# A fused Mamba, expert and attention kernel: closing norm and router gate moved to PSUM banks, and transposed sums taken first

## The chip, the cores and the metric

The kernel runs on one core of a Trainium2 chip. The metric is the device time of one execution in microseconds (us). PE is TensorE (matmuls), DVE is VectorE, ACT is ScalarE, POOL is GpSimd, and SP is SyncE, whose queue issues the DMAs.

## What is computed

The input is 8 sequences of 1024 tokens with 256 features. Four layers follow one another, each on a layer norm of its input and added to it: a Mamba block, a mixture of 16 experts, a linear attention, and the same mixture of experts again.

```python
def selective_scan(x_conv, delta, A, Bm, Cm, D_param):
    def step(h, inp):
        dA = jnp.exp(jnp.clip(dt[..., None] * A, -10.0, 0.0))
        h = dA * h + dt[..., None] * bt[:, None, :] * xt[..., None]
        hn = jnp.clip(jnp.linalg.norm(h, axis=-1, keepdims=True), 1e-06, None)
        scale = jnp.where(hn > 10.0, 10.0 / hn, jnp.ones_like(hn))
        h = jnp.where(t % 16 == 15, h * scale, h)      # the bound
        y = jnp.einsum('bn,ben->be', ct, h) + D_param * xt
...
out = (selective_scan(...) * _silu(z)) @ out_proj_w.T + out_proj_b
return layernorm(residual + out, norm_alpha, norm_bias)  # the closing norm

# mixture of experts
probs = jax.nn.softmax(logits, axis=-1)
top_p, top_i = jax.lax.top_k(probs, TOP_K)             # 6 of 16
gate = gate.at[...].add(top_p / (sum(top_p) + EPS))
for e in range(16):
    out = out + x @ expert_w[e] * gate[:, e:e + 1]
```

Of the state, 512 channels with 16 values each are carried from token to token, so the 1024 tokens of a sequence are scanned in order.

## The kernel before

The 8192 tokens are 64 tiles of 128. A first stage takes the tiles through Mamba and the first mixture; a second (`merged`) does attention and both mixtures' remaining work, 64 tiles more. The first is a software pipeline: `step(i, k, stages)` works on tile i's scan, tile i+3's input norm, projections and convolution (stage F), tile i-1's output projection and closing norm (B), tile i-2's router (X_) and tile i-3's experts (Y). Every engine runs its own `step` in the order in which the code is written, and semaphores (`M[...]` for Mamba, `R[...]` for router and experts) hold the engines together. The middle tiles run in a hardware loop.

A step has NC = 8 chunks of 16 tokens. In chunk c, DVE scans (L998, `hb<-ps_dA,hb`); ACT squares the last states (L438), and starts the decays exp(dA) of the next chunk (L432); DVE sums the squares (L1006); ACT makes the factors of the bound (L444, L447); DVE applies them (L1015, L1017, semaphore `hs`). POOL then multiplies the chunk's states with C (L362, `product`, into `prod`) and makes the inputs of the chunk after next (L370, `inputs`, into `hb`), which the scan of that chunk waits for. There are two state buffers `hb`, used in turn. PE turns the products back and adds them up (L706, `sum_states`, into bank G1 as `YT`); ACT copies the sums (L453, `copy_sums`), and PE turns them again into the bank `YP` (L714, `sums_back`), on top of D times x (L751, `skip`).

Around this skeleton each chunk carries other work: in every chunk DVE adds two experts' products to `macc` (L1083) and PE makes the next two (L740, one bank); POOL has a product of 512 columns more in chunks 1, 3 and 5 (L379, L383, L386) and the residual in 7 (L390); ACT makes the decays' arguments (L423), 5 to 11 per chunk.

What the change touches is this. **The closing norm** of tile i-1: in chunk 2 DVE adds the scaled residual to `YP` and writes the SBUF tile `oo` (L1172, `o2`), takes its statistics (L1174, L1177, L1179); in chunk 3 ACT makes the deviation by Ln and Exp (L531, L533, `sd3`), and DVE, behind most of its work of the chunk, adds epsilon, takes the reciprocal and subtracts the mean and multiplies with alpha (L1190, L1197, L1199, `o3`); in chunk 4 it multiplies and adds the bias (L1207, `o4`). **The router** of tile i-2, steps in chunks 4 to 7: the largest eight of `ex` (L1044), their match taken out of `ex` into `rest` (L1053), sums and reciprocals (L1056 to L1065), the difference `selp = ex - rest` (L1070, chunk 6), and `gate` (L1075, chunk 7). **Turning back** of tile i-1's last sums: on PE in chunk 0 behind the transposes of the input norm (L783), on ACT at the end of chunk 0, and on PE in chunk 1 behind the input projection (L794) and the router's transposes (L722).

The chunks' other small items keep their places. PE's `skip` of tile i (L751, chunk 3) writes into `YP` and waits for `o2`, since the closing norm reads that bank.

Of the kernel before, what the change touches and what calls it, by code (L numbers as in the profile page):

```python
# [22 lines left out]
ROUTER = 11  # L23
# [7 lines left out]
def build(nc, dram, out):  # L31
# [3 lines left out]
    with ctx:  # L35
# [118 lines left out]
        nf = trio[:, ST * SL + 16:ST * SL + 16 + EB]  # L154
        G = (G0, G1)
# [252 lines left out]
        def _(a):  # L408
# [65 lines left out]
            def route_init(n, k, x, stored):  # L474

                a.wait_ge(R["router"], AHEAD + n * ROUTER + 9)
# [36 lines left out]
            def step(i, k, stages):  # L513
# [4 lines left out]
                for c in range(NC):  # L518
# [75 lines left out]
                    if c == 0 and B:  # L594
                        copy_sums(i - 1, 1)
# [99 lines left out]
        def _(pe):  # L695
# [66 lines left out]
            def step(i, k, stages):  # L762
# [10 lines left out]
                for c in range(NC):  # L773
                    if early_tile(i, c, 1) is not None:
                        if early_tile(i, c, 1) == 0:
                            pe.wait_ge(M["dtb"], AHEAD + NTILES)
                            pe.wait_ge(M["o2"], AHEAD + NTILES)
                        transposes(early_tile(i, c, 1))
                    if c == 0 and F:
                        pe.wait_ge(M["xn"], AHEAD + i + 3)  # L780
                        pe.wait_ge(M["dtb"], AHEAD + i + 2)
                        for j in range(KD):
                            last = nc.tensor.transpose(F0[:, j * P:(j + 1) * P], xn[:, j * P:(j + 1) * P], ident[:])  # L783
                        last.then_inc(M["xnT"], 1)
                    if c == 0 and B:
                        sum_states(i - 1, 3)
                    if c == 1:
                        if isinstance(i, int) and i == -2:
# [11 lines left out]
                        if B:  # L800
                            sums_back(i - 1, 1)
# [166 lines left out]
        def _(v):  # L968
# [69 lines left out]

            def route_step(n, step):
# [10 lines left out]
                elif step == 3:  # L1050
                    v.wait_ge(R["router"], AHEAD + n * ROUTER + 3)
                    settle()
                    V.match_replace(rest[:], t8[:], ex[:], 0.0).then_inc(R["router"], 1)  # L1053
                elif step == 4:
# [417 lines left out]
```

## Time and profile before

| | before |
|---|---|
| median of 3 runs | 4467.03 us (4465.48 to 4468.92) |
| profiled execution, its own time | 4467.15 us |
| span of its trace | 4465.1 us |
| busy in the span: PE, DVE, ACT, POOL | 88%, 82%, 69%, 58% |
| first and last scan (512 in all) | start at 69.8 and 2968.9 us |

The first stage therefore fills two thirds of the span: 512 scans from 69.8 to 2968.9 us are 5.67 us per chunk and 45.4 us per tile. In it DVE, ACT, POOL and PE are all busy between 86 and 95 parts in a hundred of a typical stretch; an "idle before" in a row names what ended it. In the second stage PE alone is full and POOL does nothing.

### The profile page before, as it was taken

Reading aid. Unit: us, or ns where it says so; the run is one execution under the profiler, and the core shown is the slowest. Engines: PE = TensorE matmul, PEld = TensorE weight load, DVE = VectorE, ACT = ScalarE, POOL = GpSimd, SP = SyncE. Lnnn points to the kernel's source line nnn. Section 1 sums busy time; section 2 is a strip of 40 time slices with the busy share of each in tenths; the row PEclk is TensorE's granted clock in tenths of the full one; section 3 lists DMA queues with packets and bytes.
Section 4 is the critical chain, followed back from the end, with each engine's and each line's share of the span. In section 5 each row is a group of like instructions: output and inputs, shape, how many; then the busy total and the mean of one; then the engine's idle time right before and its main releaser. Section 6 shows DMA issues by size and latency. Waiting matters only on the chain.

```text
span 4465.1 us, 71554 instructions
## 1 busy us (share of the span) xinstructions
PE 3949.8 (88%) x19008; PEld 2583.5 (58%) x19008; DVE 3659.5 (82%) x8418; ACT 3088.2 (69%) x9040; POOL 2599.0 (58%) x1284
## 2 busy tenths in 40 slices
PE   5788888888888888888888888868999999999999
PEld 5666666666666666666666666634454454454454
DVE  4899999999999999999999999974557666666676
ACT  6988888888889888889889898843333333333321
POOL 4988888888889888889888888850000000000000
PEclk8899999999999999999999999999999999999999
DMA  2111111111111111111111111110000000000000
GB/s 108 57 55 56 50 58 54 58 54 58 52 51 59 50 58 54 58 54 58 54 51 56 50 60 53 57 46 15 12 16 8 16 16 6 16 16 7 6 8 10
DMA packets 91266, 187.59 MB, mean 42 GB/s; under 512 B 15873, under 2 KB 57601, under 8 KB 90625
## 3 DMA queue, kind: packets, MB, share of 16 engines
q1 hardware_dynamic: 91136, 186.11, 12.6%
q8 instruction: 52, 0.85, 0.1%
q14 instruction: 78, 0.63, 0.0%
HBM read 168.24 MB, written 17.83 MB: 42 GB/s over the span
## 4 chain that ended last, share of the span: by engine, by line
PE 44%; issue 23%; DVE 16%; POOL 13%; ACT 2%; DVEq 1%; POOLq 0%; ACTq 0%
PE ps L740 24%; POOL prod L362 7%; DVE macc L1083 6%; PE ps L853 5%; POOL hb L370 3%; PE ps L888 3%; PE ps L870 2%; POOL xcv L386 2%; PE ps L706 2%; PE ps L846 1%; POOL u L379 1%; ACT zr L423 1%; PE ps L794 1%; PE ps_dA L888 1%; DVE xin L1194 1%
## 5 line engine op out<-in xcount | busy, mean ns | idle before, releaser
L740 PE MATMUL ps<-w_x,mxT 128*128 128x512 f32 x4096 | 1968.7, 609 | 213.2 <-DVE macc L1083 213.2
L1083 DVE SCALAR_TENSOR_TENSOR macc<-ps,gate,macc 128x256 f32<-128x256 f32 x2048 | 977.9, 478 | 509.7 <-PE ps L740 417.5
L740 PEld LDWEIGHTS ps<-w_x,mxT 128*128 128x128 f32 x4096 | 732.9, 193 | 944.1 <-issue 600.6
L998 DVE TENSOR_TENSOR_SCAN hb<-ps_dA,hb 128x1088 f32<-128x1088 f32 x512 | 1240.1, 2422 | 36.3 <-POOL hb L370 30.8
L362 POOL TENSOR_TENSOR prod<-hb,cbc 128x1024 f32<-128x1024 f32 x512 | 1122.3, 2192 | 245.0 <-DVE hb L1017 241.9
L423 ACT ACTIVATE zr<-dt,aneg 128x128 f32<-128x128 f32 x4096 | 1245.9, 387 | 0.1
L370 POOL TENSOR_TENSOR hb<-u,bbc 128x1024 f32<-128x1024 f32 x512 | 1200.1, 2344 | 75.1 <-POOL prod L362 71.1
L706 PE MATMUL ps<-ident,prod 128*128 128x128 f32 x4096 | 522.8, 284 | 8.6 <-POOL prod L362 8.6
L432 ACT ACTIVATE ps_dA<-zr 128x1024 f32<-128x1024 f32 x512 | 517.3, 1010 | 0.0
L706 PEld LDWEIGHTS ps<-ident,prod 128*128 128x128 f32 x4096 | 485.5, 147 | 13.0 <-POOL prod L362 11.3
L438 ACT ACTIVATE sq<-hb 128x64 f32<-128x64 f32 x512 | 159.0, 310 | 224.7 <-DVE hb L998 223.5
L483 ACT ACTIVATE ex<-lgt,ms 128x16 f32<-128x16 f32 x128 | 39.1, 305 | 357.1 <-DVE ms L1037 356.7
L823 PEld LDWEIGHTS ps<-xin,dcw 128*128 128x128 f32 x2048 | 245.9, 197 | 21.2 <-issue 19.2
L853 PEld LDWEIGHTS ps<-xcv,w_dt 128*128 128x128 f32 x2048 | 244.9, 196 | 1.9
L823 PE MATMUL ps<-xin,dcw 128*128 128x128 f32 x2048 | 245.8, 279 | 0.0
L853 PE MATMUL ps<-xcv,w_dt 128*128 128x128 f32 x2048 | 244.1, 278 | 0.0
L783 PE MATMUL ps<-ident,xn 128*128 128x128 f32 x128 | 29.4, 313 | 170.4 <-ACT xn L526 170.4
L794 PEld LDWEIGHTS ps<-xnT,w_in 128*128 128x128 f32 x1024 | 129.6, 199 | 32.9 <-issue 20.1
L783 PEld LDWEIGHTS ps<-ident,xn 128*128 128x128 f32 x128 | 13.3, 146 | 219.9 <-ACT xn L526 112.9
L835 PEld LDWEIGHTS ps<-xnT,w_in 128*128 128x128 f32 x1024 | 124.4, 192 | 21.3 <-issue 19.5
L888 PE MATMUL ps<-zr,prod 128*128 128x512 f32 x288 | 134.5, 593 | 0.0
L1017 DVE SCALAR_TENSOR_TENSOR hb<-ps_dA,hb 128x64 f32<-128x64 f32 x512 | 133.6, 261 | 0.0
(200 smaller groups left out, 5165.5 us busy)
## 6 DMA issues: line engine op xcount, KB each, us to landing
bbc<-bcd SPq DMA_DIRECT2D x128, 512.0 KB, 3.7
cbc<-bcd SPq DMA_DIRECT2D x128, 512.0 KB, 3.7
xt<-in_x SPq DMA_DIRECT2D x128, 128.0 KB, 3.6
x2d<-macc SPq DMA_DIRECT2D x64, 128.0 KB, 1.7
out_dram<-macc SPq DMA_DIRECT2D x64, 128.0 KB, 1.7
w_x<-in_w_x SPq DMA_DIRECT2D x1, 4096.0 KB, 15.3
hb<-x2d SPq DMA_DIRECT2D x32, 128.0 KB, 2.4
sz<-x2d SPq DMA_DIRECT2D x16, 128.0 KB, 2.2
```

The lines of the kernel that those rows point to most:

```text
L362: TT(dst, states, cc, ALU.mult).then_inc(M["prodp"], 1)
L370: TT(hb[c % 2][:].rearrange("p (e n) s -> p e n s", e=EB)[:, :, :, 1:SL], u[k][:, :, t0:t0 + CH].rearrange("p e (n s) -> p e n s", n=1).br ...
L423: last = act(zr[k][:, s, :], dt[:, s // N, :], ACT.Relu, bias=10.0, scale=aneg[:, s:s + 1])
L432: act(dA3[:, :, 1:SL], zr[k][:, :, c * CH:(c + 1) * CH], ACT.Exp, bias=-10.0).then_inc(M["dA"], 1)
L706: last = mm(YT[:, h * P:(h + 1) * P], prod[h % 2][:, n, :, :].rearrange("p e t -> p (e t)"), ident[:], start=(h % 2 == 0 and n == 0), stop ...
L740: last = mm(banks[p % len(banks)][:], mxT[k][:, j, :], w_x[:, j, p * 512:(p + 1) * 512], start=(j == 0), stop=(j == KD - 1))
L794: last = mm(F0[:, m * P:(m + 1) * P], w_in[:, j, m * P:(m + 1) * P], xnT[:, j, :], start=(j == 0), stop=(j == KD - 1))
L823: last = mm(F0[:, e * P:(e + 1) * P], dcw[:, e * TAPS + t, :], xin[:, e, t:t + P], start=False, stop=(e == EB - 1 and t == TAPS - 1))
L853: last = mm(F0[:, m * P:(m + 1) * P], w_dt[:, e, m * P:(m + 1) * P], xcv[k][:, e, :], start=False, stop=(m == EB - 1 and e == EB - 1))
L888: last = mm(QUAD[s % 4][:], w_a[:, w, kk, j * P:(j + 1) * P], xTa[:, kk, g * TG:(g + 1) * TG], start=(kk == 0), stop=(kk == KD - 1))
L998: V.tensor_tensor_scan(states, dA, states, 0.0, ALU.mult, ALU.add).then_inc(M["scan"], 1)
L1083: STT(macc[k][:], banks[(e // 2) % len(banks)][:, (e % 2) * D:(e % 2 + 1) * D], gate[k][:, e:e + 1], macc[k][:], ALU.mult, ALU.add).then_i ...
```

## The change

Three groups of edits. (1) The sum, the centred and scaled form and the statistics of the closing norm live in the first 256 columns of the bank `YP` (`closing`), and only the last form goes to SBUF (`oo`). The centred form is made in chunk 2, before the bound; the last form right behind the scan of chunk 3. PE's `skip` waits for `o4` in place of `o2`, and the wait for `x1` moves to the last form. (2) For tiles whose router runs beside the scans (`beside_mamba`, tiles 0 to 61), match, difference and gate move together to the end of chunk 7, and `rest` and `selp` live in the bank F0 (`rest_p`, `selp_p`), behind the clipping of the bank into `dtt` (L1259); the router's semaphore counts change with it, and PE's next writer of F0 waits for the gate. (3) PE makes tile i-1's last sums before the transposes of the input norm and turns them back first in chunk 1; ACT copies them right behind the bound's factors of chunk 0; `sum_states(i, 0)` stands before `skip`. The product with C stands where it stood, behind the bound.

```diff
+        rest_p, selp_p = F0[:, 0:X + 2], F0[:, 32:32 + X]
+        closing = YP[:, 0:D]
...
@@ ACT step
                     if S_:
                         norms(i, c)
+                    if c == 0 and B:
+                        copy_sums(i - 1, 1)
                     if c == 0 and X_:
                         route_norm(i - 2)
...
-                    if c == 0 and B:
-                        copy_sums(i - 1, 1)
...
@@ PE step
+                    if c == 0 and B:
+                        sum_states(i - 1, 3)
                     if c == 0 and F:
                         pe.wait_ge(M["xn"], AHEAD + i + 3)
                         pe.wait_ge(M["dtb"], AHEAD + i + 2)
+                        pe.wait_ge(R["router"], AHEAD + (i - 2) * ROUTER)
...
-                    if c == 0 and B:
-                        sum_states(i - 1, 3)
                     if c == 1:
+                        if B:
+                            sums_back(i - 1, 1)
...
                     if c == 3 and S_:
-                        pe.wait_ge(M["o2"], AHEAD + (i if B else 0))
+                        sum_states(i, 0)
+                        pe.wait_ge(M["o4"], AHEAD + (i if B else 0))
                         pe.wait_ge(M["xcv"], AHEAD + i + 1)
                         skip(i, k)
-                        sum_states(i, 0)
...
@@ DVE router
+                    V.match_replace(rest_p if beside_mamba(n) else rest[:], t8[:], ex[:], 0.0).then_inc(R["router"], 1)
...
+                    TT(selp_p, ex[:, 0:X], rest_p[:, 0:X], ALU.subtract).then_inc(R["router"], 1)
...
-                TS(gate[k][:], selp[:], ms[:, 9:10], None, ALU.mult).then_inc(R["router"], 1)
+                TS(gate[k][:], selp_p if beside_mamba(n) else selp[:], ms[:, 9:10], None, ALU.mult).then_inc(R["router"], 1)
...
@@ DVE chunk 2
-                    v.wait_ge(M["x1"], AHEAD + i - 1)
-                    STT(oo[:], xt[1][:], r1b[1 - k][:], YP[:, 0:D], ALU.mult, ALU.add).then_inc(M["o2"], 1)
+                    STT(closing, xt[1][:], r1b[1 - k][:], YP[:, 0:D], ALU.mult, ALU.add).then_inc(M["o2"], 1)
...
+                    STT(closing, closing, mv[:, 2, 0:1], ga_row[:], ALU.subtract, ALU.mult).then_inc(M["o3"], 1)
                 end(2)
...
@@ DVE chunk 3
+                if S_:
+                    scan(i, k, 3)
+                if B:
+                    v.wait_ge(M["sd3"], AHEAD + i)
+                    TS(sc[:, 11:12], sc[:, 10:11], 1e-6, None, ALU.add).then_inc(M["se3"], 1)
+                    v.wait_ge(M["se3"], AHEAD + i)
+                    V.reciprocal(sc[:, 12:13], sc[:, 11:12]).then_inc(M["r3"], 1)
+                    v.wait_ge(M["r3"], AHEAD + i)
+                    v.wait_ge(M["o3"], AHEAD + i)
+                    v.wait_ge(M["x1"], AHEAD + i - 1)
+                    STT(oo[:], closing, sc[:, 12:13], be_row[:], ALU.mult, ALU.add).then_inc(M["o4"], 1)
+                behind_scan(3)
...
-                    STT(oo[:], oo[:], mv[:, 2, 0:1], ga_row[:], ALU.subtract, ALU.mult).then_inc(M["o3"], 1)
                 end(3)
...
@@ DVE chunk 4
-                    STT(oo[:], oo[:], sc[:, 12:13], be_row[:], ALU.mult, ALU.add).then_inc(M["o4"], 1)
...
@@ DVE chunk 7
+                if F:
+                    v.wait_ge(M["dtb"], AHEAD + i + 3)
+                router(7, 8)
                 if X_:
+                    route_selection(i - 2)
                     route_gate(i - 2, k)
```

The order of the instructions shows the places. First DVE in chunk 3 of a middle tile, before, from behind `macc` to the centred form (`lgt` and `mx` are the router's logits and their maximum, `xin` the convolution's input, `sc` the norm's small values):

```order
L1030 TENSOR_TENSOR lgt<-ps,rb_row 128x16
L1006 TENSOR_REDUCE nrs<-sq 128x4
L1035 MAX mx<-lgt 128x8
L1036 REGISTER_ALU
L1037 TENSOR_SCALAR ms<-mx 128x1
L1190 TENSOR_SCALAR sc<-sc 128x1
L1192 REGISTER_ALU
L1194 TENSOR_TENSOR xin<-ps,b_in 128x4x128
L1197 RECIPROCAL sc<-sc 128x1
L1199 SCALAR_TENSOR_TENSOR oo<-oo,mv,ga_row 128x256
```

The same place in the change, from the last work of chunk 2 on (`ps<-ps,mv,ga_row` is the centred form in the bank):

```order
L1190 TENSOR_SCALAR sc<-mv 128x1
L1191 SCALAR_TENSOR_TENSOR ps<-ps,mv,ga_row 128x256
L1018 SCALAR_TENSOR_TENSOR hb<-ps_dA,hb 128x64
L1020 SCALAR_TENSOR_TENSOR hb<-ps_dA,hb 128x64
L997 REGISTER_ALU
L1001 SCALAR_TENSOR_TENSOR hb<-ps_dA,hb 128x1088
L1198 TENSOR_SCALAR sc<-sc 128x1
L1200 RECIPROCAL sc<-sc 128x1
L1204 SCALAR_TENSOR_TENSOR oo<-ps,sc,be_row 128x256
L1090 REGISTER_ALU
L1091 REGISTER_ALU
L1092 SCALAR_TENSOR_TENSOR macc<-ps,gate,macc 128x256
```

The two small operations and the last form now follow the scan with nothing between them and stand before `macc`; the centred form stands before the bound of chunk 2.

Second, DVE at the end of chunk 6, before:

```order
L1006 TENSOR_REDUCE nrs<-sq 128x4
L1064 REGISTER_ALU
L1065 TENSOR_SCALAR ms<-ms 128x1
L1069 REGISTER_ALU
L1070 TENSOR_TENSOR selp<-ex,rest 128x16
L1015 SCALAR_TENSOR_TENSOR hb<-ps_dA,hb 128x64
L1017 SCALAR_TENSOR_TENSOR hb<-ps_dA,hb 128x64
```

And the end of chunk 7, before:

```order
L1006 TENSOR_REDUCE nrs<-sq 128x4
L1259 TENSOR_SCALAR sg<-ps 128x512
L1074 REGISTER_ALU
L1075 TENSOR_SCALAR gate<-selp,ms 128x16
L1015 SCALAR_TENSOR_TENSOR hb<-ps_dA,hb 128x64
L1017 SCALAR_TENSOR_TENSOR hb<-ps_dA,hb 128x64
```

The end of chunk 7 in the change (there the difference is gone from chunk 6):

```order
L1009 TENSOR_REDUCE nrs<-sq 128x4
L1269 TENSOR_SCALAR sg<-ps 128x512
L1071 MATCH_REPLACE ps<-t,ex 128x18
L1075 REGISTER_ALU
L1077 TENSOR_TENSOR ps<-ex,ps 128x16
L1083 REGISTER_ALU
L1084 TENSOR_SCALAR gate<-ps,ms 128x16
L1018 SCALAR_TENSOR_TENSOR hb<-ps_dA,hb 128x64
L1020 SCALAR_TENSOR_TENSOR hb<-ps_dA,hb 128x64
```

Match, difference and gate now follow one another behind the clipping of bank F0 (`sg<-ps`), each reading what the one before it wrote.

Third, PE from the head of a middle tile, before:

```order
L783 MATMUL ps<-ident,xn 128x128 x2
L220 ISA
L706 MATMUL ps<-ident,prod 128x128 x16
L738 ISA
L740 MATMUL ps<-w_x,mxT 128x512 x2
L791 ISA
L794 MATMUL ps<-xnT,w_in 128x128 x8
L719 REGISTER_ALU
L720 REGISTER_ALU
L722 MATMUL ps<-ident,mxn 128x128 x2
L712 ISA
L714 MATMUL ps<-ident,yT 128x128 x2
```

And in the change:

```order
L708 MATMUL ps<-ident,prod 128x128 x16
L784 REGISTER_ALU
L785 REGISTER_ALU
L786 ISA
L788 MATMUL ps<-ident,xn 128x128 x2
L740 ISA
L742 MATMUL ps<-w_x,mxT 128x512 x2
L714 ISA
L716 MATMUL ps<-ident,yT 128x128 x2
```

The sums of tile i-1 (`ps<-ident,prod`) lead the tile, and their turning back (`ps<-ident,yT`) precedes the input projection.

## Rows read from the trace of the kernel before

**Rows 1.** Groups of DVE's instructions, 600 to 2900 us

```profile
L1070 DVE TENSOR_TENSOR selp<-ex,rest 128x16 f32<-128x16 f32 x51 | 102.5, 2009 | 0.0
...
L1207 DVE SCALAR_TENSOR_TENSOR oo<-oo,sc,be_row 128x256 f32<-128x256 f32 x50 | 83.6, 1673 | 0.0
L1199 DVE SCALAR_TENSOR_TENSOR oo<-oo,mv,ga_row 128x256 f32<-128x256 f32 x50 | 51.3, 1026 | 1.8
L1075 DVE TENSOR_SCALAR gate<-selp,ms 128x16 f32<-128x16 f32 x51 | 44.9, 880 | 0.0
...
L1172 DVE SCALAR_TENSOR_TENSOR oo<-xt,r1b,ps 128x256 f32<-128x256 f32 x50 | 23.7, 474 | 0.0
...
L1030 DVE TENSOR_TENSOR lgt<-ps,rb_row 128x16 f32<-128x16 f32 x50 | 8.2, 164 | 0.0
```

**Rows 2.** The same view of 3000 to 4400 us, where POOL is idle

```profile
L1075 DVE TENSOR_SCALAR gate<-selp,ms 128x16 f32<-128x16 f32 x62 | 14.5, 234 | 2.1
...
L1070 DVE TENSOR_TENSOR selp<-ex,rest 128x16 f32<-128x16 f32 x61 | 10.0, 165 | 0.0
```

**Rows 3.** Groups of POOL's instructions, 600 to 2900 us

```profile
L370 POOL TENSOR_TENSOR hb<-u,bbc 128x1024 f32<-128x1024 f32 x404 | 946.9, 2344 | 59.1 <-POOL prod L362 55.7
L362 POOL TENSOR_TENSOR prod<-hb,cbc 128x1024 f32<-128x1024 f32 x403 | 883.6, 2192 | 194.8 <-DVE hb L1017 192.3
...
L379 POOL TENSOR_TENSOR u<-dt,xcv 128x512 f32<-128x512 f32 x50 | 63.8, 1276 | 0.0
```

**Rows 4.** Waits, 600 to 2900 us: total, times, longest

```profile
ACT sq L438 <- DVE hb L998: 162.3, 181, 1.4
...
DVE sg L1162 <- PE ps L714: 36.4, 50, 1.2
```

**Rows 5.** Timeline of DVE, one tile: the scans of chunks 0 to 7 and the next

```profile
2023.10 2.42 DVE L998 TENSOR_TENSOR_SCAN hb<-ps_dA,hb 128x1088 f32<-128x1088 f32 x1
...
2028.07 2.42 DVE L998 TENSOR_TENSOR_SCAN hb<-ps_dA,hb 128x1088 f32<-128x1088 f32 x1
...
2033.13 2.42 DVE L998 TENSOR_TENSOR_SCAN hb<-ps_dA,hb 128x1088 f32<-128x1088 f32 x1
...
2038.86 2.42 DVE L998 TENSOR_TENSOR_SCAN hb<-ps_dA,hb 128x1088 f32<-128x1088 f32 x1 [0.56 <-POOL hb L370]
...
2045.24 2.42 DVE L998 TENSOR_TENSOR_SCAN hb<-ps_dA,hb 128x1088 f32<-128x1088 f32 x1
...
2051.53 2.42 DVE L998 TENSOR_TENSOR_SCAN hb<-ps_dA,hb 128x1088 f32<-128x1088 f32 x1
...
2056.53 2.42 DVE L998 TENSOR_TENSOR_SCAN hb<-ps_dA,hb 128x1088 f32<-128x1088 f32 x1
...
2063.24 2.42 DVE L998 TENSOR_TENSOR_SCAN hb<-ps_dA,hb 128x1088 f32<-128x1088 f32 x1
...
2068.38 2.41 DVE L998 TENSOR_TENSOR_SCAN hb<-ps_dA,hb 128x1088 f32<-128x1088 f32 x1
```

**Rows 6.** Timeline of ACT, the same tile: squares of chunks 7, 0, 1, 3 to 7

```profile
2020.46 0.32 ACT L438 ACTIVATE sq<-hb 128x64 f32<-128x64 f32 x1 [1.26 <-DVE hb L998]
...
2025.63 0.31 ACT L438 ACTIVATE sq<-hb 128x64 f32<-128x64 f32 x1
...
2031.12 0.31 ACT L438 ACTIVATE sq<-hb 128x64 f32<-128x64 f32 x1
...
2041.32 0.31 ACT L438 ACTIVATE sq<-hb 128x64 f32<-128x64 f32 x1 [0.15 <-DVE hb L998]
...
2047.70 0.32 ACT L438 ACTIVATE sq<-hb 128x64 f32<-128x64 f32 x1 [1.18 <-DVE hb L998]
...
2053.98 0.32 ACT L438 ACTIVATE sq<-hb 128x64 f32<-128x64 f32 x1 [0.78 <-DVE hb L998]
...
2058.98 0.31 ACT L438 ACTIVATE sq<-hb 128x64 f32<-128x64 f32 x1
...
2065.70 0.32 ACT L438 ACTIVATE sq<-hb 128x64 f32<-128x64 f32 x1 [1.27 <-DVE hb L998]
```

More of the change, by code:

```diff
@@ L474, in route_init @@
             def route_init(n, k, x, stored):
-                a.wait_ge(R["router"], AHEAD + n * ROUTER + 9)
+                a.wait_ge(R["router"], AHEAD + n * ROUTER + 8)
                 stored()
@@ L1037, in route_scores, with beside_mamba @@
                 TS(ms[:, 2:3], mx8[:, 0:1], -1.0, None, ALU.mult).then_inc(R["nm"], 1)
+            def beside_mamba(n):
+                return not isinstance(n, int) or n < NTILES - 2
             def route_step(n, step):
@@ L1050, in route_step @@
                 elif step == 3:
[L1051 to L1054, printed above, removed]
                     v.wait_ge(R["router"], AHEAD + n * ROUTER + 4)
                     TS(ms[:, 6:7], ms[:, 3:4], 1e-10, ms[:, 5:6], ALU.mult, ALU.add).then_inc(R["router"], 1)
+                elif step == 4:
+                    v.wait_ge(R["router"], AHEAD + n * ROUTER + 5)
+                    TS(ms[:, 7:8], ms[:, 6:7], 1e-10, ms[:, 5:6], ALU.mult, ALU.max).then_inc(R["router"], 1)
@@ L1057, in route_step @@
                 elif step == 5:
                     v.wait_ge(R["router"], AHEAD + n * ROUTER + 6)
-                    TS(ms[:, 7:8], ms[:, 6:7], 1e-10, ms[:, 5:6], ALU.mult, ALU.max).then_inc(R["router"], 1)
+                    V.reciprocal(ms[:, 8:10], ms[:, 6:8]).then_inc(R["router"], 1)
                 elif step == 6:
                     v.wait_ge(R["router"], AHEAD + n * ROUTER + 7)
-                    V.reciprocal(ms[:, 8:10], ms[:, 6:8]).then_inc(R["router"], 1)
+                    TS(ms[:, 12:13], ms[:, 5:6], ms[:, 8:9], 1e-10, ALU.mult, ALU.mult).then_inc(R["router"], 1)
@@ L1063, in route_step @@
                 elif step == 7:
-                    v.wait_ge(R["router"], AHEAD + n * ROUTER + 8)
-                    TS(ms[:, 12:13], ms[:, 5:6], ms[:, 8:9], 1e-10, ALU.mult, ALU.mult).then_inc(R["router"], 1)
+                    settle()
+                    V.match_replace(rest_p if beside_mamba(n) else rest[:], t8[:], ex[:], 0.0).then_inc(R["router"], 1)
             def route_selection(n):
-                v.wait_ge(R["router"], AHEAD + n * ROUTER + 5)
-                TT(selp[:], ex[:, 0:X], rest[:, 0:X], ALU.subtract).then_inc(R["router"], 1)
+                v.wait_ge(R["router"], AHEAD + n * ROUTER + 9)
@@ L1072, in route_gate @@
+                if beside_mamba(n):
+                    TT(selp_p, ex[:, 0:X], rest_p[:, 0:X], ALU.subtract).then_inc(R["router"], 1)
+                else:
+                    TT(selp[:], ex[:, 0:X], rest[:, 0:X], ALU.subtract).then_inc(R["router"], 1)
             def route_gate(n, k):
                 v.wait_ge(R["router"], AHEAD + n * ROUTER + 10)
-                TS(gate[k][:], selp[:], ms[:, 9:10], None, ALU.mult).then_inc(R["router"], 1)
+                TS(gate[k][:], selp_p if beside_mamba(n) else selp[:], ms[:, 9:10], None, ALU.mult).then_inc(R["router"], 1)
@@ L1217, in step @@
                 start(5)
+                router(3, 4)
+                halfway(5)
                 router(4, 5)
-                halfway(5)
-                router(5, 6)
                 if F:
@@ L1234, in step @@
                     V.bn_aggr(mv[:, 0, :], st[:, 0, :]).then_inc(M["mv1"], 1)
-                router(6, 7)
+                router(5, 6)
                 if L_:
@@ L1240, in step @@
                 halfway(6)
-                router(7, 8)
-                if X_:
-                    route_selection(i - 2)
+                router(6, 7)
                 end(6)
```

20 lines of the change are left out of this document (5 added, 15 removed).

## The prediction

> **What bounds the kernel now.** I read the page's busy slices first: the first stage, 45.4 us per tile, has DVE, ACT, POOL and PE nearly full at once, so no single busy share names the bound. The second stage has PE full and POOL idle. Then I read DVE's groups in the first stage [rows 1]. Four of them are odd. The difference of 128x16 elements takes 2.009 us on the mean, a gate of the same size 0.880, the two norm forms of 128x256 take 1.673 and 1.026. A form of the same shape with one input in a PSUM bank takes 0.474 (L1172), and a 128x16 operation with one input in a bank takes 0.164 (L1030). In the second stage, with POOL idle, the same difference takes 0.165 and the same gate 0.234 [rows 2]. So the four instructions lose time only when POOL works, and only where all their tensor inputs lie in SBUF: 1.84 + 0.65 + 1.20 + 0.55 = 4.24 us per tile in which DVE stands behind a POOL instruction.
>
> Next, whether anyone waits for DVE there. POOL waited 192.3 us in all for the bound's second operation [rows 3], and ACT 162.3 us for the scan [rows 4]. The window holds 403 chunks, 50.4 tiles, so that is 3.8 and 3.2 us per tile. DVE sets the pace on the mean, but with the others close: without waits for it, POOL would need 45.4 - 3.8 = 41.6 us per tile and ACT 45.4 - 3.2 = 42.2.
>
> The timelines show where. The scans [rows 5] give DVE's chunk lengths: 4.97, 5.06, 5.73, 6.38, 6.29, 5.00, 6.71, 5.14 for chunks 0 to 7, together 45.28 us. The long ones are 3, 4 and 6, which hold three of the four instructions. In chunk 2's length 0.56 is a wait for POOL ahead of scan 3. ACT waits 1.18 ahead of the squares of chunk 4, 0.78 ahead of 5, 1.27 ahead of 7, hardly elsewhere [rows 6].
>
> **The change part by part.** *What it removes.* In this tile the four instructions take 1.29 (chunk 3), 1.43 (4), 2.00 (6) and 0.87 (7), by subtraction the same 5.59 as their means. In their place stand forms with at most one SBUF input. The two norm forms take the price of L1172, 0.47 each, one in chunk 2 and one in chunk 3. The difference takes that of L1030, 0.16. The gate now reads a bank, and lies between 0.16 (L1030) and 0.23 [rows 2]; I take 0.2. No row shows DVE writing such a result into a bank. Below, such a write could be as cheap as to SBUF; above, I let each of the four that write a bank cost 0.1 more, the spread of the two prices just given rounded up, 0.4 per tile. I take the lower end, because L1172 and L1030 already pay for the access to a bank in the other direction. Net, DVE loses 5.59 - 1.3 = 4.3 us of work per tile.
>
> *What it moves.* The small operations L1190 and L1197 lay around `xin`; now the addition, the reciprocal and the last form follow one another, each waiting for the one before, right behind scan 3. No row here gives the gap of such a chain; between nothing and the 0.16 of a small operation for each of two gaps I take 0.3 in all. The match (about 0.15, near L1030) leaves chunk 4 for chunk 7, where it, the difference and the gate wait for one another and for the clipping: 0.35 more by the same price. So DVE's lengths become: chunk 2, 5.73 - 0.56 + 0.47 = 5.6; chunk 3, 6.38 - 1.29 + 0.47 + 0.3 = 5.9; chunk 4, 6.29 - 1.43 - 0.15 = 4.7; chunk 6, 4.7; chunk 7, 5.14 - 0.87 + 0.2 + 0.16 + 0.15 + 0.35 = 5.15; the rest stay. Their sum is 41.1, below POOL's 41.6 and ACT's 42.2. DVE stops being the bound, and the saving is cut off by the other two.
>
> *The sums first.* DVE's product with z (L1162) waited 36.4 us for the sums turned back, 0.7 per tile [rows 4]. I credit nothing for its removal: behind it stands the bound of chunk 1, for which ACT's factors are late too, since ACT reached the squares of chunk 1 at 2031.12, 0.63 after scan 1 had ended (2028.07 + 2.42) [rows 5, 6]. If that cover is wrong, it is 0.7 more per tile. The price of the move is that ACT's copy stands right behind the factors of chunk 0 and may wait for POOL's last product and PE's sums, with the router's norm, the input norm's scaling and decays queued behind it. PE's `skip` now waits for `o4`, with the experts' pair 3 and the convolution queued behind it, and DVE's `macc` of chunk 4 behind these; that pair could not start before `macc` 3 anyway, and `o4` now stands ahead of `macc` 3 on DVE, so I price it at nothing and keep it for the range. The first writer of F0 waits for the gate, which was done at the end of the tile before.
>
> *The sum.* ACT's own lengths are 5.49 (chunk 0), 10.70 (3 and 4 together, 12.66 less the waits 1.18 and 0.78), 5.00 (5), 5.45 (6) and 5.17 (7) [rows 6]. POOL's are 2.34 + 2.19 + 0.14 (55.7/404) = 4.67, and 1.28 more in chunks 1, 3 and 5 [rows 3]. With two state buffers one engine may be about a chunk ahead of another, so I let the longest of the three decide over pairs of chunks. Pairs 0+1, 2+3, 4+5, 6+7, before: 10.63 (POOL), 11.55, 11.29, 11.85 = 45.3, against 45.28 measured. After: 10.63, 11.5, 10.63, 10.62 (ACT) = 43.4, a gain of 1.9. Pairs 7+0, 1+2, 3+4, 5+6, before: 10.66, 10.63, 12.67, 11.71 = 45.7; after: 10.66, 10.66, 10.70, 10.63 = 42.65, a gain of 3.0. I take the middle, 2.4 per tile. 62 tiles have their norm and router beside POOL's work: 2.4 x 62 = 149 us. The second stage keeps its SBUF tiles and has PE as its bound: nothing. The profiled execution took 4467.15 us (span 4465.1), as the median (4467.03) does, so 4467 - 149 = 4318 us.
>
> *A rule weighed.* In the second stage an all-SBUF difference takes 0.165 and L1030, which reads a bank, 0.164 [rows 1, 2]: no surcharge. The Trainium skill, VectorE: DVE Perf Modes, section on the TRN2 errata, gives DVE a fixed 120 cycles for a source in PSUM and 58 for one in SBUF; by it the five operations that newly read a bank would cost 65 ns more each, an estimate of 0.3 us per tile or 20 us, and the time would be 4338.
>
> **Rivals.** *Stiff coupling (4447 us).* If no engine may run ahead, the longest of the three decides in every single chunk: 5.49 (ACT), 5.95 (POOL), 5.6, 5.95, 5.50 (ACT's chunk 4, 6.28 less 0.78), 5.95, 5.45, 5.17 = 45.1, which leaves 0.3 per tile, 20 us. Against it: before, the same count gives 5.49 + 5.95 + 5.95 + 6.38 + 6.29 + 5.95 + 6.71 + 5.17 = 47.9, and 45.3 was measured. Cases between it and mine, which lose up to half of the gain to waits for `sd3`, the copy or `skip`, reach 4395.
>
> *The floor (4269 us).* The waits for DVE vanish wholly and ACT's 42.2 is reached: 3.2 x 62 = 198 us. That needs ACT never to wait for POOL's long chunks.
>
> *The forms still wait.* If what holds DVE is not its SBUF inputs but any access beside POOL, nothing changes and 4467 stays. L1172 at 0.474 speaks against it.
>
> *Slower: the closing chain holds DVE behind scan 3.* ACT makes `sd3` only behind z's three operations and five decays of chunk 2, just ahead of its squares of chunk 3, where it waited 0.15 for scan 3 [rows 6], so `sd3` came barely in time. If ACT falls back in chunks 0 to 2 behind the copy, all of its lateness now falls on DVE ahead of `macc`, and by `skip` on PE. It decides from 2.4 us per tile; at 3.0 the loss would be 0.6 x 62 = 37 us, 4504. It would need ACT to be half a chunk late in every tile.
>
> **How the numbers follow.** Chances: my forecast, with its own range 4280 to 4365, 0.70; stiff or half-eaten, 4365 to 4447, 0.13; the floor, under 4280, 0.06; no change 0.04; slower 0.07. The predicted time is 4318. The range goes from 4278 to 4395, which takes in the unknown price of writes to a bank (0.4 x 62 = 25 us), the 0.7 of L1162, and half of the gain eaten. What a measurement here can tell from no change is 0.2%, 9 us: faster 0.89, same 0.04, slower 0.07.
>
> **What would show it.** In the changed kernel's trace, the two forms near 0.47, the difference near 0.16 and the gate near 0.2, in the first stage too; scans every 5.3 to 5.4 us on the mean; scan 3 to scan 4 at 5.9, scan 6 to scan 7 below 5.6; POOL's waits for the bound below 2 us per tile and ACT's for the scan below 1. It is wrong if the four stay long, if DVE's first small operation behind scan 3 waits over 1 us for ACT, or if PE's `skip` makes `macc` of chunk 4 wait.

## The result: 4388.4 us, the right direction, with half of the gain gone elsewhere

The changed kernel takes 4388.43 us (median of 4, 4387.47 to 4389.72), the kernel before 4466.99 in the same rounds: a ratio of 0.9824, with a 95% interval of 0.9807 to 0.9841, or 78.6 us less. The forecast was 4318 us within 4278 to 4395. The last scan starts at 2891.1 us in place of 2968.9, so the whole gain of 78 us lies in the first stage, as the sum had it. But it is 1.2 us per tile and not 2.4. One of the four runs of the router-only kernel below fell in a slower state (5081 us at a mean granted clock of 0.747) and is left out of its time.

| | before | after |
|---|---|---|
| span of the profiled execution | 4465.1 us | 4387.3 us |
| first and last scan start | 69.8, 2968.9 us | 70.6, 2891.1 us |
| per tile between them | 45.4 us | 44.2 us |
| mean granted clock of PE over the span | 0.979 | 0.967 |

The four instructions did what the forecast said. The groups of DVE in the changed kernel, 600 to 2850 us, in the columns of [rows 1]:

```profile
L1204 DVE SCALAR_TENSOR_TENSOR oo<-ps,sc,be_row 128x256 f32<-128x256 f32 x51 | 24.7, 484 | 2.2
L1191 DVE SCALAR_TENSOR_TENSOR ps<-ps,mv,ga_row 128x256 f32<-128x256 f32 x51 | 24.6, 482 | 0.0
...
L1084 DVE TENSOR_SCALAR gate<-ps,ms 128x16 f32<-128x16 f32 x50 | 11.7, 234 | 1.8
...
L1077 DVE TENSOR_TENSOR ps<-ex,ps 128x16 f32<-128x16 f32 x50 | 8.9, 179 | 1.7
...
L1071 DVE MATCH_REPLACE8 ps<-t,ex 128x18 f32<-128x18 f32 x50 | 8.5, 170 | 0.0
```

The norm forms take 0.484 and 0.482 us, the difference 0.179, the gate 0.234, where [rows 1] had 1.673, 1.026, 2.009 and 0.880. Here a result written into a bank costs hardly more than one written to SBUF (0.179 against the 0.165 of [rows 2]): the lower bound was right. 4.2 us of DVE's work per tile are gone.

The four instructions also stand in new places, so the place might have freed them and not the bank. In six to seven tiles between 1000 and 1300 us, however, POOL is at work on its inputs all through the last form, the difference and the gate, as in this tile:

```profile
1193.16 2.33 POOL L372 TENSOR_TENSOR hb<-u,bbc 128x1024 f32<-128x1024 f32 x1 [0.17 <-POOL prod L364]
```

```profile
1193.56 0.48 DVE L1204 SCALAR_TENSOR_TENSOR oo<-ps,sc,be_row 128x256 f32<-128x256 f32 x1
```

For these three it is the bank. The centred form (L1191) runs mostly in a gap of POOL's work (two of seven lie wholly beside it, and take 0.48 too), so for it the new place may have done a part.

The waits of the same stretch, in the columns of [rows 4]:

```profile
POOL prod L364 <- DVE hb L1020: 130.6, 218, 2.3
PE ps L708 <- POOL prod L364: 104.9, 50, 2.3
PE ps L753 <- DVE oo L1204: 104.0, 51, 2.2
...
ACT yT L455 <- PE ps L708: 57.2, 49, 1.8
...
ACT nrl L446 <- DVE nrs L1009: 44.6, 52, 0.9
...
ACT sq L440 <- DVE hb L1001: 39.3, 84, 1.3
...
DVE xcv L1226 <- PE ps L826: 32.1, 50, 2.1
DVE hb L1018 <- ACT ps_dA L449: 30.5, 102, 0.7
```

ACT's wait for the scan fell from 3.2 to 0.8 us per tile (39.3 us over 50.8 tiles), as forecast; POOL's for the bound from 3.8 to 2.6 only, where below 2 was forecast, and the scans start every 5.5 us on the mean and not every 5.3 to 5.4. New are three waits: ACT's copy of the sums for PE (1.1 us per tile), PE's `skip` for the last norm form (2.0), and DVE's `xcv` for PE's convolution (0.6). Each was a candidate for the missing 1.2 us per tile, and none had a price in the sum.

The tiles are not alike, and that led to the cause. Two neighbours in the timeline of DVE, the changed kernel: the scans of their chunks 0, 1 and 2, and of the next tile's chunk 0.

```profile
1130.95 2.42 DVE L1001 TENSOR_TENSOR_SCAN hb<-ps_dA,hb 128x1088 f32<-128x1088 f32 x1 [0.22 <-issue]
...
1135.90 2.42 DVE L1001 TENSOR_TENSOR_SCAN hb<-ps_dA,hb 128x1088 f32<-128x1088 f32 x1
...
1140.95 2.42 DVE L1001 TENSOR_TENSOR_SCAN hb<-ps_dA,hb 128x1088 f32<-128x1088 f32 x1
...
1174.10 2.42 DVE L1001 TENSOR_TENSOR_SCAN hb<-ps_dA,hb 128x1088 f32<-128x1088 f32 x1
...
1178.99 2.42 DVE L1001 TENSOR_TENSOR_SCAN hb<-ps_dA,hb 128x1088 f32<-128x1088 f32 x1
...
1185.07 2.42 DVE L1001 TENSOR_TENSOR_SCAN hb<-ps_dA,hb 128x1088 f32<-128x1088 f32 x1
...
1220.01 2.42 DVE L1001 TENSOR_TENSOR_SCAN hb<-ps_dA,hb 128x1088 f32<-128x1088 f32 x1 [0.22 <-issue]
```

The first tile takes 43.15 us, close to what the forecast's sum gives (43.0). The second takes 45.91. Its chunk 1 (1178.99 to 1185.07) is 1.0 us longer than its neighbour's, since `macc` waits for PE's pair; its chunk 4 (1196.49 to 1203.47) is 1.7 us longer (5.29 in the neighbour), since `xcv` waits for PE's convolution. These are the waits, `xcv` of the first tile ahead of the two of the second:

```profile
1156.92 0.69 DVE L1226 TENSOR_SCALAR xcv<-ps 128x512 f32<-128x512 f32 x1 [0.43 <-PE ps L826]
...
1182.15 1.00 DVE L1092 SCALAR_TENSOR_TENSOR macc<-ps,gate,macc 128x256 f32<-128x256 f32 x2 [0.74 <-PE ps L742]
...
1202.47 0.69 DVE L1226 TENSOR_SCALAR xcv<-ps 128x512 f32<-128x512 f32 x1 [2.11 <-PE ps L826]
```

PE at the two heads, the same kernel:

```profile
1133.22 1.97 PE L708 MATMUL ps<-ident,prod 128*128 128x128 f32 x16 [2.28 <-POOL prod L364]
...
1135.24 1.88 PE L742 MATMUL ps<-w_x,mxT 128*128 128x512 f32 x4
```

```profile
1176.43 2.89 PE L708 MATMUL ps<-ident,prod 128*128 128x128 f32 x16 [1.94 <-POOL prod L364]
...
1179.54 2.47 PE L742 MATMUL ps<-w_x,mxT 128*128 128x512 f32 x4
```

The same sixteen transposes take 1.97 us in one tile and 2.89 in the other, and the same experts' pair 1.88 and 2.47. Both follow an idle time of about 2 us. What differs is the clock. Windows of 4 us of the changed kernel, at the heads of these two tiles and in chunk 3 of the second; PEclk is the share of the full clock that was granted:

```profile
core 0: us, PE busy (x) PEld busy (x) DVE busy (x) ACT busy (x) POOL busy (x), PEclk, DMA share, GB/s
...
1131.50:1135.50 4.00, 2.28 (x19) 2.22 (x20) 3.69 (x9) 3.31 (x10) 3.86 (x2) 1.00 0.66 200
1174.50:1178.50 4.00, 2.07 (x14) 2.07 (x15) 3.78 (x8) 3.67 (x11) 3.83 (x2) 0.85 0.70 199
1192.00:1196.00 4.00, 2.07 (x11) 1.90 (x10) 3.68 (x11) 3.02 (x12) 3.83 (x3) 0.80 0.10 36
```

In the first tile PE keeps 1.00, 2.4 GHz. In the second it is granted 0.85 at the head and 0.80 in chunk 3, a mix of 2.4 and 1.2 GHz, beside the two places where PE waits for POOL's last product and for the last norm form. The kernel before had the same at some of its heads, behind its wait for the input norm. That wait, 600 to 2900 us, 2.4 us in each tile, and windows of 4 us at three heads:

```profile
PE ps L783 <- ACT xn L526: 122.7, 50, 2.5
```

```profile
1019.50:1023.50 4.00, 2.40 (x14) 2.40 (x15) 3.69 (x11) 3.59 (x12) 3.65 (x3) 0.78 0.71 238
1065.50:1069.50 4.00, 2.19 (x19) 2.20 (x20) 3.69 (x10) 3.58 (x12) 3.86 (x2) 1.00 0.73 226
1111.00:1115.00 4.00, 2.38 (x17) 2.38 (x18) 3.70 (x11) 3.59 (x12) 3.65 (x3) 0.86 0.67 200
```

Its tiles take 45.3 us where the head keeps 1.00 and 46.2 where it does not. The tile of [rows 5] was one of the undisturbed ones.

This holds for every tile. Windows of 0.5 us over the stage show where the granted clock falls below the full 2.4 GHz (a fall, from here on). Of the 47 whole tiles of the changed kernel between 600 and 2750 us, the 11 without a fall take 43.1 to 43.4 us, the 32 with one fall 44.2 to 45.0, and the 4 with two falls 45.7 to 46.0. Of the 46 of the kernel before, 29 have none (45.3 to 45.4) and 17 have one (46.1 to 46.3).

### The profile page after: what moved, and what is told of

It reads as the page before. It is cut to its first block, busy times and chain, and to the rows that moved or that the text cites. A ratio compares the mean times of both kernels' runs of the same rounds, so it can differ in the third digit from the quotient of the medians.

```text
span 4387.3 us, 71595 instructions
## 1 busy us (share of the span) xinstructions
PE 3958.2 (90%) x19008; PEld 2614.2 (60%) x19008; DVE 3466.3 (79%) x8418; ACT 3078.2 (70%) x9040; POOL 2593.1 (59%) x1284
## 4 chain that ended last, share of the span: by engine, by line
PE 51%; ACT 13%; POOL 12%; DVE 12%; issue 12%; DVEq 0%; POOLq 0%; ACTq 0%
PE ps L742 23%; POOL prod L364 8%; ACT zr L425 6%; PE ps L826 5%; PE ps L856 5%; PE ps L708 4%; DVE macc L1092 3%; PE ps L891 3%; PE ps L873 2%; POOL hb L372 2%; PE ps L753 2%; POOL xcv L388 2%; PE ps L849 1%; DVE hb L1001 1%; PE ps_dA L891 1%
## 5 line engine op out<-in xcount | busy, mean ns | idle before, releaser
L1001 DVE TENSOR_TENSOR_SCAN hb<-ps_dA,hb 128x1088 f32<-128x1088 f32 x512 | 1240.7, 2423 | 58.6 <-POOL hb L372 47.9
L708 PE MATMUL ps<-ident,prod 128*128 128x128 f32 x4096 | 551.2, 293 | 139.3 <-POOL prod L364 139.3
L708 PEld LDWEIGHTS ps<-ident,prod 128*128 128x128 f32 x4096 | 505.7, 151 | 226.0 <-POOL prod L364 189.5
L753 PE MATMUL ps<-xcv,ddp 128*128 128x128 f32 x512 | 81.5, 307 | 132.2 <-DVE oo L1204 132.2
L1018 DVE SCALAR_TENSOR_TENSOR hb<-ps_dA,hb 128x64 f32<-128x64 f32 x480 | 126.1, 263 | 47.3 <-ACT ps_dA L449 46.6
L753 PEld LDWEIGHTS ps<-xcv,ddp 128*128 128x128 f32 x512 | 68.7, 209 | 147.2 <-DVE oo L1204 80.0
L446 ACT ACTIVATE nrl<-nrs 128x4 f32<-128x4 f32 x512 | 101.4, 198 | 64.5 <-DVE nrs L1009 54.2
L1009 DVE TENSOR_REDUCE nrs<-sq 128x4 f32<-128x64 f32 x512 | 108.0, 211 | 39.4 <-ACT sq L440 38.0
L799 PE MATMUL ps<-xnT,w_in 128*128 128x128 f32 x1024 | 134.0, 287 | 4.5 <-ACT xnT L552 4.5
```

What stands on the lines that cost most here:

```text
L708: last = mm(YT[:, h * P:(h + 1) * P], prod[h % 2][:, n, :, :].rearrange("p e t -> p (e t)"), ident[:], start=(h % 2 == 0 and n == 0), stop ...
L753: mm(YP[:].rearrange("p (h e t) -> p e h t", h=4, e=EB)[:, e, :, :], ddp[:, e, :], xcv[k][:, e, :].rearrange("p (h t) -> p h t", h=4), sta ...
L1001: V.tensor_tensor_scan(states, dA, states, 0.0, ALU.mult, ALU.add).then_inc(M["scan"], 1)
```

## The experiments

Three theories stood against each other. **A**: ACT's copy, early in chunk 0, waits for PE's sums and makes ACT late. **B**: PE's `skip` waits for the last norm form and holds what is queued behind it. **C**: PE's idle time at the tile's head and in chunk 3 lets its clock fall to half, and the slow stretch behind it delays chunk 1 or 4. Each comparison is with the kernel before in the same rounds.

### One group at a time

**Forms only**: the change without its third group.

```diff
@@ ACT step
-                    if c == 0 and B:
-                        copy_sums(i - 1, 1)
                     if c == 0 and X_:
                         route_norm(i - 2)
...
+                    if c == 0 and B:
+                        copy_sums(i - 1, 1)
...
@@ PE step
-                    if c == 0 and B:
-                        sum_states(i - 1, 3)
                     if c == 0 and F:
...
+                    if c == 0 and B:
+                        sum_states(i - 1, 3)
                     if c == 1:
-                        if B:
-                            sums_back(i - 1, 1)
...
+                        if B:
+                            sums_back(i - 1, 1)
```

`sum_states(i, 0)` stays ahead of `skip`.

> The change without its third group: PE makes and turns back the last sums, and ACT copies them, where the kernel before did; norm and router stay in the banks. Theory A (the missing half of the gain went into ACT's copy, which now waits 1.1 us per tile for PE's sums and makes ACT late in chunk 1): the copy no longer waits, and the time is 4330 to 4370 us, faster than the change's 4388. Rival B (PE's skip, which waits 2 us per tile for the last norm form, sets the time): that wait stays, and without the earlier sums the time is 4388 to 4415.

Measured: 4381.96 us, ratio 0.9808 (0.9792 to 0.9824). Neither: it is 6 us faster than the change, not 20 to 60 (A), and not slower (B). The copy's wait is gone from ACT, and the time hardly moves. 45 of 47 tiles have a fall of the clock here.

**Order only**: the kernel before with the third group alone, and the first sums ahead of `skip`.

```diff
+                    if c == 0 and B:
+                        copy_sums(i - 1, 1)
                     if c == 0 and X_:
                         route_norm(i - 2)
...
+                    if c == 0 and B:
+                        sum_states(i - 1, 3)
                     if c == 0 and F:
                         pe.wait_ge(M["xn"], AHEAD + i + 3)
...
                     if c == 1:
+                        if B:
+                            sums_back(i - 1, 1)
```

> The kernel before with only the third group (sums made first, copied early, turned back first, and the first sums ahead of skip). Theory A: a loss, 4475 to 4520 us, since the copy's wait makes ACT late while DVE still stands behind POOL. Rival B: a gain of up to the 0.7 us per tile of DVE's wait for the sums turned back, 4425 to 4467.

Measured: 4467.24 us, ratio 1.0002 (0.9992 to 1.0012). No loss and no gain: A is missed, and B's range ends where nothing is gained. The third group is worth nothing by itself, as the forecast priced it.

**Router only**: match, difference and gate in the bank at the end of chunk 7, on the kernel before, with PE's wait for the gate ahead of the transposes of the input norm.

```diff
+                    V.match_replace(rest_p if beside_mamba(n) else rest[:], t8[:], ex[:], 0.0).then_inc(R["router"], 1)
...
+                    TT(selp_p, ex[:, 0:X], rest_p[:, 0:X], ALU.subtract).then_inc(R["router"], 1)
...
+                TS(gate[k][:], selp_p if beside_mamba(n) else selp[:], ms[:, 9:10], None, ALU.mult).then_inc(R["router"], 1)
```

> The kernel before with only the router's match, difference and gate in the bank. It frees 1.8 + 0.65 us of DVE per tile. If DVE's saving passes on until ACT and POOL cut it off, the gain is 1.1 to 1.3 us per tile: 4385 to 4400 us (both theories; it says how much of the gain the router alone carries).

Measured: 4415.62 us (median of 3), ratio 0.9883 (0.9863 to 0.9903): 51 us, 0.8 per tile. The expected 4385 to 4400 us is missed by 16 us.

**Closing norm only**: on the kernel before, with the first sums ahead of `skip`.

```diff
+                    STT(closing, closing, mv[:, 2, 0:1], ga_row[:], ALU.subtract, ALU.mult).then_inc(M["o3"], 1)
...
+                    STT(oo[:], closing, sc[:, 12:13], be_row[:], ALU.mult, ALU.add).then_inc(M["o4"], 1)
...
+                        sum_states(i, 0)
+                        pe.wait_ge(M["o4"], AHEAD + (i if B else 0))
```

> The kernel before with only the closing norm in the bank, its last form behind scan 3, and the first sums ahead of skip, which waits for the last form. Theory A: gain of 1.0 to 1.3 us per tile, 4385 to 4405 us, since skip's wait is hidden behind the experts' pair. Rival B: skip's wait eats it, 4430 to 4480.

Measured: 4391.96 us, ratio 0.9833 (0.9816 to 0.9849): 75 us. That lies in A's range and outside B's, so B falls here. But 51 and 75 together give 85 (forms only), not 126: the two do not add up, and something cuts them off.

### Filling PE's idle time

The clock can be tested nearly by itself: matmuls that nothing reads, put into the idle time, keep PE busy and can otherwise only delay it. `fill` writes a bank that is free at the place and is overwritten afterwards; the reads are of resident weights, so the output does not depend on it. The first edit is at the head of a tile, the second in chunk 3. Each brings waits of PE with it; no run has these waits without the matmuls.

```diff
+            def fill(count, bank=F0):
+                for _ in range(count):
+                    mm(bank[:], ident[:], w_dt[:, 0, :], start=True, stop=True)
...
+                    if c == 0 and F and X_:
+                        pe.wait_ge(M["dtb"], AHEAD + i + 2)
+                        pe.wait_ge(R["router"], AHEAD + (i - 2) * ROUTER)
+                        fill(2)
...
                     if c == 3 and S_:
+                        if F and X_:
+                            pe.wait_ge(M["yt"], AHEAD + i * 2)
+                            fill(2, YT)
                         sum_states(i, 0)
```

**The kernel before, filled at the head** (without the wait for the router, which it has no use for).

> The kernel before with the two filling matmuls at the head. Its clock falls at 22 tile heads of 52, and its tiles take 45.3 or 46.2 us. Theory C: the falls go away, all tiles take 45.3, and the time is 4430 to 4450 us. If the filling itself delays the first expert pair: 4465 to 4490.

Measured: 4447.35 us, ratio 0.9954 (0.9938 to 0.9971). Its windows of the stage, 600 to 2700 us:

```profile
600.00:2700.00 2100.00, 1880.46 (x10930) 1361.04 (x10930) 1995.99 (x4027) 1887.25 (x5697) 1878.01 (x928) 1.00 0.17 56
```

The granted clock is 1.00 in place of 0.99, and every tile takes 45.3 us. More work on PE made the kernel 20 us faster: the kernel before had paid that much to its clock.

**The change, filled at the head.**

> The change with two matmuls of 128x512 from resident weights into the free bank F0 (about 1.8 us of PE, overwritten afterwards) at the head of a tile, where PE waits 1.9 to 2.3 us for POOL's last product. Nothing of the result depends on them. Theory C (PE's clock falls to half at the tile's head in most tiles of the change, behind that idle time, and the slow transposes and pair make ACT's copy and DVE's macc of chunk 1 late: tiles with the fall take 44.3 to 44.9 us, tiles without it 43.1): the granted clock of the stage rises from 0.97 to 0.99 or more, the tiles take 43.1 to 43.4 us, and the time is 4315 to 4335 us. Rival A (the copy's place alone): more work on PE can only delay, 4388 to 4420. Rival B (skip's wait for the last norm form): no change, 4388.

Measured: 4388.84 us, ratio 0.9824 (0.9808 to 0.9841). The time did not move, and A and B seemed to be right. The windows say otherwise. Head and chunk 3 of three tiles of this kernel:

```profile
1040.50:1044.50 4.00, 3.43 (x22) 2.36 (x21) 3.72 (x7) 3.31 (x10) 3.86 (x2) 1.00 0.51 178
1057.50:1061.50 4.00, 2.17 (x10) 1.65 (x11) 3.79 (x12) 3.11 (x12) 3.83 (x3) 0.82 0.24 72
1085.50:1089.50 4.00, 3.78 (x23) 2.60 (x22) 3.78 (x9) 3.66 (x11) 3.83 (x2) 1.00 0.60 194
1102.50:1106.50 4.00, 2.55 (x10) 2.04 (x11) 3.81 (x14) 3.09 (x12) 3.83 (x3) 0.74 0.19 62
1130.50:1134.50 4.00, 3.44 (x22) 2.41 (x21) 3.69 (x9) 3.31 (x10) 3.86 (x2) 1.00 0.65 190
1147.50:1151.50 4.00, 2.33 (x12) 1.62 (x13) 3.79 (x13) 3.11 (x13) 3.83 (x3) 1.00 0.20 74
```

The heads are at 1.00 throughout. Now the clock falls in chunk 3 (0.82, 0.74), behind PE's wait for the last norm form, and where it does not (1.00) the tile is short: the three take 44.9, 45.0 and 43.2 us. The fall had moved from one idle time to the next.

**Forms only, filled at the head.**

> The change without its third group (as in the forms-only run, 4382 us, in which every tile's head fell to half clock), with the same two filling matmuls at the head, where PE waits for the input norm. Theory C: 4300 to 4335 us. Rival A and B: 4382 to 4420. Beside the filled change it says what the third group is worth when the clock stays up: nothing to 20 us either way.

Measured: 4386.56 us, ratio 0.9818 (0.9802 to 0.9835). C's time is missed here too, and the picture is the same, with the same mean clock of 0.97: no fall at the head, one in chunk 3 in 32 of 47 tiles.

**The change, filled in chunk 3 alone.**

> The change with the filling in chunk 3 alone. Theory C: the clock falls at the head, as in the change, in most tiles: 4375 to 4395 us. Rival B: if chunk 3 alone mattered, 4315 to 4345.

Measured: 4378.52 us, ratio 0.9797 (0.9780 to 0.9813), as C had it. The mean clock of the stage is 0.97; 32 of 47 tiles still have a fall, all of them at the head. One place alone gives 10 us.

**The change, filled at both.**

> The change with two filling matmuls at the head of a tile and two more in chunk 3, ahead of the first sums, in the bank that the sums then overwrite. With the filling at the head alone the clock no longer fell there but in chunk 3, beside PE's wait of 2 us for the last norm form, and the time stayed at 4389; tiles without a fall took 43.1 us. Theory C: no fall is left, all tiles take 43.1 to 43.4 us, and the time is 4315 to 4340 us. Rival B (skip's wait for the last form costs by itself, not by the clock): the wait's effect stays, 4375 to 4395.

Measured: 4323.45 us, ratio 0.9677 (0.9660 to 0.9693). Windows of the stage of this kernel, and of the changed kernel unfilled behind it:

```profile
600.00:2700.00 2100.00, 2022.60 (x11665) 1455.86 (x11666) 1931.57 (x4232) 1975.44 (x5972) 1968.81 (x971) 1.00 0.18 58
```

```profile
600.00:2700.00 2100.00, 1869.93 (x10976) 1405.35 (x10975) 1885.96 (x4117) 1922.93 (x5821) 1917.65 (x947) 0.97 0.17 56
```

The granted clock is 1.00 against 0.97, no tile between 600 and 2750 us has a fall, and the tiles take 43.2 and 43.4 us in turn, as the tiles without a fall do in the unfilled change. That agreement also speaks against the waits of the filling as the cause. Its waits, 600 to 2750 us:

```profile
POOL prod L364 <- DVE hb L1032: 70.4, 149, 0.7
...
ACT sq L440 <- DVE hb L1013: 32.3, 75, 1.0
...
DVE xcv L1238 <- PE ps L838: 22.2, 50, 0.5
...
PE ps L708 <- POOL prod L364: 19.3, 49, 0.6
...
PE ps L753 <- DVE oo L1216: 16.3, 50, 0.5
```

POOL's wait for the bound is down to 1.4 us per tile (70.4 over 49.8 tiles), which the forecast wanted below 2. PE still waits at the head (19.3 us) and for the last form (16.3 us), but a fifth or a sixth as long as unfilled (104.9 and 104.0).

**Forms only, filled at both.**

> The change without its third group, with the same filling at both places. Theory C: 4315 to 4345 us. The difference to the filled change is what the third group is worth once the clock stays up: I expect the filled change to be 0 to 15 us faster, since DVE's product with z waits for the sums turned back in this one.

Measured: 4320.49 us, ratio 0.9676 (0.9660 to 0.9692). So the third group is worth nothing with the clock up, too; I had expected 0 to 15 us for it.

This also settles the savings that did not add up. In tiles without a fall, router only takes 44.7 us on the mean (34 tiles) and closing norm only 43.8 (23), against 45.3 before: 0.65 and 1.5 us saved, 2.15 together. With the clock up, forms only takes 43.2, which is 2.1 less. At full clock the two savings add up almost wholly; the 40 us that were missing are the falls.

### Two moves on the changed kernel

**Copy late**: ACT's copy back at the end of chunk 0, PE as in the change.

```diff
-                    if c == 0 and B:
-                        copy_sums(i - 1, 1)
                     if c == 0 and X_:
                         route_norm(i - 2)
...
                     if G_ and c < NC - 1:
                         decays(i + 1, 1 - k, DECAYS[c], DECAYS[c + 1])
...
+                    if c == 0 and B:
+                        copy_sums(i - 1, 1)
```

> The change with ACT's copy of the last sums put back to the end of chunk 0 (PE's order as in the change). Rival A: ACT no longer waits, 4340 to 4370 us. Theory C: the clock still falls at the head, the wait only moves to PE's turning back, now queued ahead of the input projection: 4380 to 4410.

Measured: 4393.88 us, ratio 0.9836 (0.9819 to 0.9852). A's range is missed: ACT no longer waits there, and PE waits for the copy in its stead. Its 19 tiles without a fall take 43.6 to 43.9 us, 0.6 more than in the change on the mean, so this place of the copy has a cost of its own; there are fewer falls (29 of 48 tiles), and the time comes out only 5 us above the change.

```profile
PE ps L716 <- ACT yT L455: 53.3, 48, 1.5
```

**Skip late**: `skip` behind the experts' pair of chunk 3.

```diff
                     if c == 3 and S_:
                         sum_states(i, 0)
+                    if c == 4 and S_:
                         pe.wait_ge(M["o4"], AHEAD + (i if B else 0))
                         pe.wait_ge(M["xcv"], AHEAD + i + 1)
                         skip(i, k)
```

> The change with PE's skip behind the experts' pair of chunk 3, ahead of the convolution, so that pair 3 does not queue behind the wait for the last norm form. Rival B: the pair comes earlier, 4350 to 4380 us. Theory C: pair 3 waits for macc of chunk 3 anyway, the idle time grows and skip comes later, and the clock falls as before: 4385 to 4425 us.

Measured: 4430.31 us, ratio 0.9916 (0.9900 to 0.9933), slower than both theories said, 42 us above the change. The waits of this kernel, 600 to 2700 us:

```profile
PE ps L742 <- DVE macc L1093: 174.2, 94, 3.0
...
DVE xcv L1227 <- PE ps L827: 81.9, 46, 4.3
```

Pair 3 waits for `macc` of chunk 3, which comes later than the last form; the idle time grows to as much as 3.0 us, `skip` and the convolution queue behind it, and `xcv` of chunk 4 waits 1.8 us per tile (81.9 us over 46.8 tiles). The 28 tiles without a fall take 44.0 to 44.2 us, 0.9 more than in the change, so here the place costs by itself; the 19 with a fall take 45.2 to 47.3. That `skip` used to fill a part of this idle time is my reading of it; no run tests it apart.

## Why the forecast held its range and missed its middle

**What bounds the kernel** and **what the change removes** were right. The four instructions were held by POOL, and three of them are shown to be free for their bank alone (for the centred form bank and place are not told apart); that cost 4.2 us of DVE per tile, and it went. The rule of the Trainium skill that was weighed, VectorE: DVE Perf Modes, section on the TRN2 errata, is not borne out by these rows: the norm forms from a bank take 0.484 and 0.482, where the same forms, all in SBUF, took 0.483 and 0.474 at their shortest in the kernel before; 65 ns more each does not show.

**The sum over pairs of chunks** was near for a tile at full clock: it gave 43.0 us, and tiles without a fall take 43.1 to 43.4. Some of that is chunks cancelling out. In the change filled at both places, chunks 0+1 take 10.0 us and 4+5 take 10.3, where the sum had 10.63 for each, and 6+7 take 11.35 where it had 10.62. Chunk 6 is the one that was off, 5.9 us where below 5.6 was named: scan 7 waits 0.60 for POOL's inputs in a typical one, and the bound of chunk 6 waits 0.36 for ACT's factors (`DVE hb L1018 <- ACT ps_dA L449` in the waits above).

**The step that failed** is in *The sums first*: "so I price it at nothing and keep it for the range", of PE's wait ahead of `skip`, and with it the silence on PE's wait at the head. As waits they cost little, as the filled kernels show: PE is busy in both places and the time is 4323. What they cost is the clock. PE was counted as a fourth engine with time to spare, whose durations stay the same when the others get faster. In the kernel before it had one idle time of 2.4 us per tile, and its clock fell behind it in 17 of 46 tiles; the change made a second in chunk 3 (2.0 us), kept one at the head (2.1 us), and has falls in 36 of 47. The fall stretches the transposes and the pair by up to a half, ACT's copy and `macc` of chunk 1 wait for them (or `xcv` of chunk 4 for the convolution), and the tile takes 44.2 to 46.0 us. The sign that was named for it, `macc` of chunk 4 waiting, was the wrong place: it is `macc` of chunk 1 and `xcv` of chunk 4 that wait.

The account, in medians: 4388.4 to 4323.5 us, 65 us, is what the clock costs the changed kernel, and 4467.1 to 4447.4, 20 us, what it cost the kernel before. With the clock held up in both, the change is worth 4447.4 - 4323.5 = 124 us, 2.0 per tile; the forecast had 149. The 25 us between them lie on both sides of the sum. It had 45.5 us per tile before (the middle of 45.3 and 45.7), where tiles without a fall take 45.3, and 43.0 after, where they take 43.25 on the mean. Its starting point, 4467, held the 20 us of falls that the filled kernels do not have. So it is in part luck that 4318 lies so near to the filled kernel's 4323: 20 us too much at the start and 25 too much taken off.

**The rivals.** Stiff coupling did not happen, nor the floor. "Half-eaten" at up to 4395 is where the time came out, but not by the waits named for it as such: undoing the copy makes the kernel 5 us slower, and the wait for `sd3` is 4.0 us in all over 51 tiles. That the range held is therefore luck as far as the cause goes: the clock was not among its reasons. (In the check of stiff coupling on the kernel before, chunk 2 stands at 5.95 us where the rows give 5.73; it is 47.7 and not 47.9, and the argument stays.) What was named as the slower case, ACT's lateness falling on DVE behind scan 3, is not seen.

**A rule that bears on it.** The Trainium skill, TensorE: Matmul & The Clock Gate, section Why this matters for your kernels, says to leave no idle gaps beyond a length that it names between bursts of matmuls, if the throughput is not to drop in mid-kernel. PE's longest wait between 600 and 2750 us is 2.5 us in the kernel before and 2.3 in the change, shorter than that length, so by this rule the clock would have stayed up. The rows show otherwise, and they decide: with waits of 1.9 to 2.3 us at two places the clock fell in 36 of 47 tiles of the change, and it fell in none of 49 with both places filled. That keeping PE busy helps, the runs do bear out.

**What stays open.** Why the clock falls behind one idle time and not behind the next of the same length (2.28 us of waiting in the tile that kept 1.00, 1.94 in the one that lost it) is not settled by these runs. Nor is there a run with the filling's waits and no matmuls. Whether useful work can stand where the filling stands was tried only with `skip`, which made it worse.

## What to carry to other kernels

When a change makes the other engines faster, ask what PE does with the time: an idle time that costs nothing as a wait can cost the clock, and the slow stretch behind it lies where the next matmuls are awaited. Filling it with matmuls that nobody reads tells this from a wait, once every such place is filled, and here it is the fastest version as well (4320 to 4323 us against 4467). If a fix of one place moves nothing, look at the granted clock of the next place before giving up the theory: one fill alone gave 0 and 10 us, both together 65. Sorting the tiles by whether the clock fell in them shows the cost without any further run.

Beside POOL, a DVE instruction with all inputs in SBUF can take twelve times as long as its work (2.009 us for 0.165). For the last form, the difference and the gate, one tensor input in a PSUM bank was enough to free it (0.484, 0.179 and 0.234 us while POOL worked).

## What was not expected of the hardware

A stage can settle into a pattern of falls. Forms-only alternates between 44.0 and 44.7 us tile by tile with a fall in nearly every one, closing-only between 43.8 without a fall and 44.9 with one, and the change filled at the head repeats three tiles of 44.9, 45.0 and 43.2 us. Of two savings of 51 and 75 us that touch different chunks, 40 us were lost when both were made, and the filling gave them back.
